# Attention of image 1 with 32 value columns in four column groups, and its row sums by way of GpSimd additions

## The reference, cut to what matters

```
g = layernorm(x)                       # per image and channel
q, k, v = w1 g + b1, w2 g + b2, w3 g + b3
scores = q^T k                         # 4096 x 4096 per image
probs  = exp(scores - rowmax(scores))
out    = (probs v) / (probs 1)         # 32 channels, and one sum per query
x      = x + g + out
```

## Time and profile before

| | |
|---|---|
| time, median of 3 runs | 1299.03 us (1297.82 to 1301.66) |
| profiled execution: span | 1557.5 us |
| profiled execution: own time beside its span | the page gives none |
| TensorE busy | 1255.7 us (81%) |
| VectorE busy | 993.9 us (64%) |
| ScalarE busy | 662.7 us (43%) |
| GpSimd busy | 485.1 us (31%), nothing after 1160 us |
| mean granted TensorE clock | 0.875 |
| attention of image 1 in the profile | 1252.7 us to the end |

### The profile page before, as it was taken

The page is one execution under the profiler, slowest core; times in us unless marked ns, Lnnn a source line. Parts: engine busy times, 40 slices in busy tenths (PEclk is TensorE's granted clock), DMA queues, the critical chain, the costliest instruction groups (busy, mean ns, idle before and its releaser), DMA issues.

```text
span 1557.5 us, 20328 instructions
## 1 busy us (share of the span) xinstructions
PE 1255.7 (81%) x7126; PEld 508.6 (33%) x7126; DVE 993.9 (64%) x1679; ACT 662.7 (43%) x882; POOL 485.1 (31%) x537
## 2 busy tenths in 40 slices
PE   5999977387879888672587767876889999999996
PEld 1888843143423333220122222222222222222221
DVE  5899988253635544463464647665687777777772
ACT  5777766243424433111032322332346544444444
POOL 6000000746464565474655354654400000000000
PEclk9999978688988988755587779888999999999999
DMA  2655401543332331111111111111000000000000
GB/s 55 156 121 119 105 1 55 170 124 104 100 99 94 100 104 36 34 44 34 44 36 36 28 39 30 40 37 30 29 0 1 0 1 14 1 0 0 0 0 14
DMA packets 59672, 79.21 MB, mean 51 GB/s; under 512 B 12230, under 2 KB 43974, under 8 KB 59414
## 3 DMA queue, kind: packets, MB, share of 16 engines
q1 hardware_dynamic: 44342, 47.03, 11.6%
q0 software_dynamic: 15264, 31.29, 7.1%
HBM read 70.94 MB, written 7.34 MB: 50 GB/s over the span
## 4 chain that ended last, share of the span: by engine, by line
PE 58%; DVE 16%; another core or an unknown queue 12%; issue 9%; ACT 3%; SPq 1%; DVEq 1%; DMA 0%; ACTq 0%
PE psum L1971 11%; PE psum L1833 9%; PE psum L1953 9%; PE psum L1994 7%; PE psum L1718 5%; DVE maxes L1144 4%; DVE probs_and_weighted L881 3%; PE psum L1733 3%; PE psum L1668 2%; PE psum L1916 2%; PE psum L1745 2%; PE psum L1843 1%; PE psum L2000 1%; PE psum L1805 1%
## 5 line engine op out<-in xcount | busy, mean ns | idle before, releaser
L554 POOL DMA_INDIRECT tile_data<-quad_table,index_u x477 | 461.4, 967 | 626.0 <-DMA quad_table<-quad_rows_or_splits 245.2
L1144 DVE TENSOR_REDUCE maxes<-psum 128x1 f32<-128x512 f32 x512 | 331.1, 683 | 172.7 <-PE psum L1953 108.5
L1574 ACT ACTIVATE quads<-psum 128x1024 f32<-128x1024 f32 x256 | 248.2, 1021 | 329.8 <-PE psum L2000 214.8
L1971 PE MATMUL psum<-quads 128*64 128x512 f32 x1024 | 277.1, 637 | 0.0
L1833 PE MATMUL psum<-scratch,quad_rows_or_splits 128*128 128x512 f32 (+1 forms) x486 | 233.8, 626 | 33.2 <-DVE scratch L966 23.4
L1953 PE MATMUL psum<-products_or_attention 128*128 128x512 bf16 x256 | 101.5, 452 | 134.4 <-DVE maxes L1144 123.3
L1994 PE MATMUL psum<-quads,probs_and_weighted 32*128 32x512 f32 x1024 | 159.8, 696 | 2.6 <-ACT quads L1574 1.8
L1833 PEld LDWEIGHTS psum<-scratch,quad_rows_or_splits 128*128 128x128 f32 x486 | 96.3, 211 | 146.6 <-issue 126.4
L978 DVE TENSOR_TENSOR probs_and_weighted<-psum,quads 128x512 f32<-128x512 f32 (+1 forms) x81 | 50.6, 640 | 145.6 <-remote 80.2
L1433 ACT ACTIVATE vals<-psum 96x384 f32<-96x384 f32 x53 | 25.8, 487 | 222.9 <-remote 96.6
L1953 PEld LDWEIGHTS psum<-products_or_attention 128*128 (+1 forms) x256 | 20.8, 99 | 266.4 <-DVE maxes L1144 176.3
(11 more groups left out here) (227 smaller groups left out, 1464.9 us busy)
## 6 DMA issues: line engine op xcount, KB each, us to landing
products_or_attention<-positions SPq DMA_DIRECT2D x30, 576.0 KB, 8.2
products_or_attention<-bands SPq DMA_DIRECT2D x12, 768.0 KB
tile_data<-quad_table,index_u POOLq DMA_INDIRECT x477
quads<-bands SPq DMA_DIRECT2D x6, 768.0 KB
quad_table<-quad_rows_or_splits SPq DMA_DIRECT2D x4, 768.0 KB, 5.6
products_or_attention<-bands SPq DMA_DIRECT2D x4, 576.0 KB
quad_table<-quad_rows_or_splits SPq DMA_DIRECT2D x2, 640.0 KB, 7.3
products_or_attention<-positions SPq DMA_DIRECT2D x4, 288.0 KB, 7.0
```

Of the source, the lines that this page charges most:

```text
L554: pool.indirect_dma_start(out=out[:, k * CORNERS * C:(k + 1) * CORNERS * C], out_offset=None, in_=table, in_offset=bass.IndirectOffsetOnAx ...
L1144: v.reduce_max(maxes[:, tile_of_q, block_of_k:block_of_k + 1], psum[:, FREE + c % 2, :], AXIS_X)\
L1574: act.activation(probs[:, s % 2, 2 * BLK * h:2 * BLK * (h + 1)], psum[:, SCORES + 2 * h:SCORES + 2 * h + 2, :].rearrange("p a n -> p (a n) ...
L1971: last = pe.matmul(psum[2 * C * h:2 * C * h + 2 * C, SUMS, :], f3[b][:, 4 * s + i, :], probs[:, s % 2, BLK * i:BLK * i + BLK], start=s == ...
```

## The change

Only image 1 is touched.

- `weigh`: each of the four key tiles' products now has a 32-column weight (values only) and its own column group (32 i). The halves and the chunks between them stay where they are.
- Behind the second half, eight products with a 32-column weight of ones, 128 queries wide: four column groups by two, over `pair_probs`. These are two sums of two key tiles each, which GpSimd adds from the probabilities (one 128 x 1024 addition a step). The products wait for that addition, and `summed` is signalled behind them.
- `copy_sums` copies a third piece (128 x 128 totals); a new `move_parts` on ScalarE at step 2 brings pieces onto the same partitions in five copies. VectorE does one reciprocal of 128 x 128 in place of four of 32 x 128, and the quotient's steps are an addition (64 x 512), an addition, a product and an addition (32 x 512 each), at steps 1, 5, 6 and 7.
- The fill of the block after the next moves from step 1 to step 7 on TensorE, from step 2 to 7 on ScalarE and from step 3 to 7 on VectorE, and uses another bank, since the old one now holds the sums with ones.

```diff
+            def add_pairs(n, u):
+
+                pool.wait_ge(probs_ready, lin(n, 2, 2 * KEY_QUADS * NBLK + 2))
+                pool.wait_ge(summed, lin(n, 1, KEY_QUADS * NBLK - 1))
+                pool.tensor_tensor(pair_probs[:, u, :], probs[:, u, 0:2 * BLK], probs[:, u, 2 * BLK:4 * BLK], ALU.add)\
+                    .then_inc(pairs_added, 1)
+
+            with pool.Fori(0, KEY_QUADS * NBLK // 2) as i:
+                for u in range(2):
+                    add_pairs((i, 2, u), u)
...
+            def pair_sum_part(j, k):
...
+                if k == 0:
+                    v.wait_ge(sums_copied, lin(j, 1, NBLK + 1))
+                    v.reciprocal(inverses, totals).then_inc(sum_steps, 1)
+                    v.tensor_tensor(att_sum[:, 0, :], att_halves[:, 0, :], att_halves[:, 1, :], ALU.add).then_inc(sum_steps, 1)
+                elif k == 4:
+                    v.wait_ge(parts_moved, lin(j, 1, 1))
+                    v.tensor_tensor(num, att_sum[0:C, 0, :], upper_sum, ALU.add).then_inc(sum_steps, 1)
+                elif k == 5:
...
+                    v.tensor_tensor(quotient, num, inverse_row, ALU.mult).then_inc(sum_steps, 1)
+                elif k == 6:
...
-                    if ahead and s == (3 if b else KEY_QUADS - 1):
+                    if ahead and s == KEY_QUADS - 1:
                         read_fill(b, fill_ahead(b, j), (var, stp, start + 2))
...
-                act.activation(att_halves[:, 1, :], psum[2 * C:4 * C, SUMS, :], ACT.Identity).then_inc(sums_copied, 1)
+                last = act.activation(att_halves[:, 1, :], psum[2 * C:4 * C, SUMS, :], ACT.Identity)
+                if b:
+                    last = act.activation(totals, psum[:, SAMPLES, 0:P], ACT.Identity)
+                last.then_inc(sums_copied, 1)
+
+            def move_parts(j):
+
+                act.wait_ge(sum_steps, lin(j, PAIR_STEPS, SUM_STEPS * NBLK + 2))
+                act.activation(upper_sum, att_sum[IMAGE[1], 0, :], ACT.Identity)
+                for g in range(4):
+                    last = act.activation(inverse_row[:, P * g:P * g + P], inverses[C * g:C * g + C, :], ACT.Identity)
+                last.then_inc(parts_moved, 1)
...
+                    if s == 2 and not first and before(b, j)[0]:
+                        move_parts(before(b, j)[1])
-                    if ahead and s == (2 if b else KEY_QUADS - 1):
+                    if ahead and s == KEY_QUADS - 1:
                         take_fill(b, fill_ahead(b, j), (var, stp, start + 2))
...
+                if b:
+                    for h in range(2):
+                        i = 2 * half + h
+                        pe.matmul(psum[C * i:C * i + C, SUMS, :], f3[b][:, 4 * s + i, 0:C],
+                                  probs[:, s % 2, BLK * i:BLK * i + BLK], start=s == 0, stop=s == KEY_QUADS - 1)
+                    if half:
+                        pe.wait_ge(pairs_added, lin((var, KEY_QUADS * stp, KEY_QUADS * start + s), 1, 1))
+                        for h in range(2):
+                            for g in range(4):
+                                last = pe.matmul(psum[C * g:C * g + C, SAMPLES, 0:P], ones[:, 0:C],
+                                                 pair_probs[:, s % 2, BLK * h + P * g:BLK * h + P * g + P],
+                                                 start=s == 0 and h == 0, stop=s == KEY_QUADS - 1 and h == 1)
+                        last.then_inc(summed, 1)
+                    return
...
-                    if ahead and b == 0 and s == KEY_QUADS - 1:
-                        pe.wait_ge(maxed, lin((var, stp, start + 1), MAXIMA, MAXIMA))
+                    if ahead and s == KEY_QUADS - 1:
+                        pe.wait_ge(maxed, lin((var, stp, start + 1 + NBLK * b), MAXIMA, MAXIMA))
                         fill(b, fill_ahead(b, j), (var, stp, start + 2))
...
-                    if ahead and b and s == 1:
-                        fill(b, fill_ahead(b, j), (var, stp, start + 2))
```

More of the change, by code:

```diff
@@ L192, in build @@
         att_halves = scratch[0:2 * C, 4 * BLK:6 * BLK].rearrange("p (h n) -> p h n", h=2)
+        at = N // 2
+        pair_probs = tile_data[:, at:at + 4 * BLK].rearrange("p (u n) -> p u n", u=2)
+        at += 4 * BLK
+        totals, inverses = (tile_data[:, at + k * P:at + (k + 1) * P] for k in range(2))
+        at += 2 * P
+        upper_sum, inverse_row = (tile_data[0:C, at + k * BLK:at + (k + 1) * BLK] for k in range(2))
         band_pos, band_int, band_floor, band_no = (y_all[:, at:at + BLK] for at in (5 * CO, 5 * CO + BLK, N + 5 * CO, N + 5 * CO + BLK))
@@ L264, in build @@
         sums_copied = sem("sums_copied"); sum_steps = sem("sum_steps"); residuals = sem("residuals_added")
-        x_final = sem("x_final")
+        x_final = sem("x_final"); pairs_added = sem("pairs_added"); parts_moved = sem("sum_parts_moved")
         block = ctx.enter_context(nc.Block())
@@ L272, in build @@
         N_CONST = 16 * (9 * DEFORMS + 11)
-        NM_STEPS, SUM_STEPS = 5, 6
+        NM_STEPS, SUM_STEPS, PAIR_STEPS = 5, 6, 4
         def lin(n, scale=1, off=0):
@@ L1166, in negated @@
                     .then_inc(nm_ready, 1)
+            def pair_sum_part(j, k):
+                var, stp, start = j
+                steps_done = SUM_STEPS * NBLK
+                num, quotient = att_sum[0:C, 1, :], att_sum[IMAGE[1], 2, :]
+                if k == 0:
[6 more added lines that the diff above has]
+                elif k == 5:
+                    v.wait_ge(sum_steps, lin(j, PAIR_STEPS, steps_done + 3))
+                    v.tensor_tensor(quotient, num, inverse_row, ALU.mult).then_inc(sum_steps, 1)
+                elif k == 6:
+                    v.wait_ge(sum_steps, lin(j, PAIR_STEPS, steps_done + 4))
+                    at = lin(j, BLK)
+                    here = slice(at, at + BLK) if isinstance(at, int) else bass.ds(at, BLK)
+                    v.tensor_tensor(x_of[1][:, here], x_of[1][:, here], quotient, ALU.add).then_inc(x_final, 1)
             def sum_part(b, j, k):
+                if b:
+                    pair_sum_part(j, k)
+                    return
                 q = queries(b, j)
@@ L1602, in attention @@
                         attend(b, (0, 0, j), last=j == NBLK - 1)
-                    act.wait_ge(sum_steps, SUM_STEPS * (NBLK * B - 2) + 1)
                     copy_sums(b, (0, 0, NBLK - 1))
+                    move_parts((0, 0, NBLK - 1))
             other_quads(0, lambda: copy_offsets_0(0, 0))
```

4 lines of the change are left out of this document (3 added, 1 removed).

## The result

The change makes the kernel slower, by about as much as forecast. After: 1314.59 us (median of 4 runs, 1313.61 to 1316.59); before, run beside it: 1300.35 us (4 runs, 1297.82 to 1304.42); ratio 1.0111, 95% interval 1.0095 to 1.0126, so +14.2 us. The profiled execution has a span of 1312.8 us and took 1314.73 itself. In the traces image 1's attention, from the first scores of its first block to the end, takes 304.8 us before (1252.7 to 1557.5) and 318.7 after (994.1 to 1312.8). The 13.9 us between them are nearly the whole difference of the medians, 14.2. The 258 us by which the profile of before was too long lie outside this stage.

A forecast was written before the change was run, and what follows sets the result against it. TensorE was taken to bound image 1's attention (39.2 of 40 us busy). Five loop blocks +10.2, first block +1.2, block 6 +2.6, last block 0 and tail +1.8 gave +15.8 us: 1299.0 becomes 1314.8, range 1304 to 1336.

The forecast's parts named there:

- block 0: Image 1's first block, weighing image 0's last step in its step 0: 3.1 - 0.98 - 0.32 - 0.62 = +1.2 us.
- block 6: Image 1's block without a fill or a stall today: 3.5 - 0.98 - 0.38 + 0.5 = +2.6 us.
- the last block with the tail: End of image 1: last block 0, since the addition fits under its 3.44 us step; tail +1.8 us.
- The ones: New TensorE products behind the second half: 0.44 us a step, 3.5 in eight steps; bounds 0.2 and 1.7.
- The values: Four column groups save 0.98 us in step 7 only; elsewhere just shorter weight loads, 0.38 us a block.
- The stall: TensorE's wait for VectorE leaves step 4 (0.62 us) and moves to step 2, charged 0.5; net -0.1.
- The fill: Moved to step 7: costs TensorE 1.05 us in either place, so nothing, with 0.2 to 0.4 us of cover.
- GpSimd's 2.5 us: One 128 x 1024 addition a step on GpSimd takes 2.5 us, hidden in the seven blocks with chunks.
- GpSimd late: Rival: the addition lasts 6.4 us and steps 6.5 rather than 5.1, giving 1421 us; chance 0.07.
- The groups running past a chunk: Faster rival: second half's products run beside the first's despite the chunk between; -40 us, 1275; chance 0.06.
- The ones hidden wholly: Faster rival: products with ones hide under the second half, which leaves two groups free; -24 us, 1291; chance 0.06.
- The contention: Rival: GpSimd's addition holds VectorE's two-SBUF-input operations; at worst 49 us, a third showing +16, 1331; chance 0.10.

The follow-up runs named there:

- one_product_with_ones: The changed kernel with seven of the eight products with ones left out a step; 1307.06 us, ratio 1.0046 to the kernel before.
- two_column_groups: The changed kernel with the four value products in two column groups rather than four; 1320.73 us, ratio 1.0154 to the kernel before.
- fill_at_step_7: The kernel before with only the fill, ScalarE's copies of it and VectorE's rest moved to step 7; 1294.32 us, ratio 0.9956.
- free_groups_sums_placed: ones_in_free_groups with VectorE's three closing operations moved right behind the first reduction of steps 4, 5 and 6; 1294.75 us, ratio 0.9959 to the kernel before.
- two_additions_a_step: The changed kernel with each GpSimd addition made twice, the first into unused space; 1392.1 us, ratio 1.0702 to the kernel before.
- the small addition: ones_in_free_groups and values_chunk_ones with GpSimd adding 64 columns instead of 1024; 1292.03 us and 1274.30 us.
- ones_in_free_groups: The changed kernel with each half given the ones products of the two column groups it leaves free; 1307.02 us, ratio 1.0059 to the kernel before.
- values_chunk_ones: The changed kernel with four value products together, then one chunk, the ones, remaining chunks, in image 1; 1307.25 us, ratio 1.0062 to the kernel before.
- halves_together: The changed kernel with the chunk between the halves moved behind them, in image 1 only; 1306.39 us, ratio 1.0057 to the kernel before.

## Why the prediction was right, point by point

**The total and its sign.** Forecast +15.8 us and 1314.8, measured +14.2 and 1314.59. That the total came so close is in part luck, since errors of both signs cancel. By the traces the five loop blocks grew by 8.7 for a forecast 10.2 and block 0 by -0.3 for 1.2; block 6, and the last block with the tail, grew by 0.6 each more than forecast. The mechanism, more work on the engine that bounds the stage, holds.

**The ones, 0.44 a step, less two shorter weight loads of 0.027 each: right.** The forecast net is 0.39; steps 3, 5 and 6 grow by 0.39, 0.38 and 0.38. `one_product_with_ones` gives the 0.44 by taking it away: 5.09 to 4.65. I had half of the records slipping under the second half as a bound of 0.2 a step. Half of them do start there, but the step still grows by the time of the busiest groups, which was the term used.

**The values: nothing in seven steps, 0.98 in step 7: right in kind.** `two_column_groups` puts it at 0.85. Of the old 1.97 us in step 7, 0.10 was waiting for the maxima and not products; that part I mis-sized. In block 6 the term fails: step 7 grew by 0.07 where -0.54 was forecast (-0.98 and +0.44), because 0.53 us of what is saved is spent waiting for the parts of the maxima. In the loop blocks the moved fill covers that wait.

**The stall: right in place, slightly too dear.** It moved from step 4 to step 2, with 0.35 idle (0.41 by the steps' difference) for a forecast 0.5.

**The fill: mis-sized in my kernel's favour.** I said that it costs TensorE 1.05 in either place. It costs 0.70 at step 7, as `fill_at_step_7` shows, because it fills 0.35 us of waiting that I had not read in the earlier trace rows. The cover of 0.2 to 0.4 us for what stands behind it held: neither the row of maxima nor the fill's rest made a wait. With these, a loop block: 2.75 for the ones in steps 0 to 6, -0.44 for values and ones together in step 7, -0.35 for the fill, -0.63 and +0.41 for the stall, together +1.74 where I had +2.0.

**The first and last blocks.** Block 0 came out at 39.49 against 39.77, not +1.2. Of that, 1.48 us is step 0 alone (6.78 before, 5.30 after). In the trace of before it runs at a lower clock, as the busy time of that stretch shows:
```profile
1254.70:1258.80 4.10, 3.96 (x11) 0.72 (x11) 1.87 (x4) 1.42 (x2) 0.00 (x0) 0.59 0.01 2
```
After, the same stretch has full clock; without that the term is +1.2, as forecast. What decides it I can't say: the profiles of `two_column_groups`, `one_product_with_ones` and `free_groups_sums_placed` show 6.8 there too, those of `fill_at_step_7` and `two_additions_a_step` 5.3. Block 6 grew by 3.16 for a forecast 2.6, by its step 7. The last block and the tail grew by 2.36: the tail's 1.92 for a forecast 1.8, and 0.43 in steps 3 and 4 of the last block, which I had at nothing. 0.30 of it stays when the addition is small, so that it is `move_parts`, for which the next probabilities wait on ScalarE. The rest, 0.12 in step 4, goes with the small addition and also with a single product with ones; TensorE waits 0.63 us for GpSimd there, whose addition takes 2.83.

**GpSimd's 2.5 us: right.** 2.35 measured. The Trainium skill, GPSIMD Engine Reference, section 3.1, would make it 2.25 by half of its figure for 2048 f32; the trace is 4% above.

**The rivals.** GpSimd late did not happen in the blocks with chunks; in the last block TensorE waits for it, which I had named as a sign of being wrong, but no more than that 0.12 us comes of it before the tail. `two_additions_a_step` shows what lies beyond the deadline, and it is worse than my rule for it (1392 where 1338 was expected of that run), because VectorE is held as well. The groups running past a chunk: no, the 5.09 in both kernels with two and four groups excludes it. The ones hidden wholly: not in this order, but in another, as `ones_in_free_groups` shows. The contention was the rival that I priced wrongly in kind. Its mechanism is real, and the price is no third of anything: it is the rest of the addition at the moment when VectorE's operation starts. In the changed kernel VectorE comes first with L1205, by 0.22 us and in one block by 0.04, and pays 0.1 with L1197 (0.79 for 0.68), which starts just before an addition's end. So my forecast held by a margin that I had not worked out, and that is luck. With steps 0.4 us shorter VectorE comes second, and most of the gain of the steps is gone.

The Trainium skill, GPSIMD Engine Reference, section 1, says that GpSimd's SBUF interfaces are shared with VectorE and that VectorE's instructions with two SBUF inputs or in a 2-port mode contend. The traces agree as to two SBUF inputs: held were L1183, L1205, L1197 and L1200. With one SBUF input, the copy of the queries and a small scalar operation (L1178 of `two_additions_a_step`, 2.10 for 0.17) were held too; whether these run in a 2-port mode no run here shows. Reductions from PSUM (0.68), the reciprocal (0.94) and L1121 with one SBUF input (0.75) were not.

## What to carry to other kernels

When an idle engine is given work, list the operations of its neighbour that share its way to SBUF, and lay both out in time: what counts is not only how busy either is but which starts first, and a margin of 0.2 us is none. If a variant that should save a fixed time per step saves nothing, compare the steps one by one; here most showed the gain, and the one or two at the block's edge gave it back. Try the parts of a change by themselves: one of them, the moved fill, was a gain of 0.4% within a change that lost 1.1%.

## What was not expected of the hardware

- Some operations of VectorE that begin while GpSimd adds are held until that addition ends, however small they are: 0.23 to 2.26 us for 128 x 16, 0.68 to 2.70 for 32 x 512, 0.43 to 2.48 for a copy of 128 x 512. What it costs is the rest of the addition. An operation of 32 x 512 that begins 0.20, 1.27, 1.67 or 2.11 us into the addition takes 2.69, 1.61, 1.21 or 0.79 us, and so always ends 0.54 behind it. Where VectorE's 0.68 us start first, GpSimd's 2.35 becomes 2.67, or 2.85 if VectorE is ahead by only 0.04.
- Matmuls in column groups that are free start beside those ahead of them in the code's order, if the shape is the same (8 of 16 records with ones, 0.02 us behind the second half's first pair). Where each half has only the products with ones of the groups that it leaves free, these cost nothing (5.09 to 4.65 us a step). A product over the whole array between two groups of products ends the overlap (5.09 with two and with four groups for the values).
- A wait of 2 us on TensorE was followed by a stretch at a granted clock of 0.50 in some cases and not in others: behind two of the five waits of `ones_in_free_groups`, behind every such wait of `values_chunk_ones`, and behind none in the loop blocks of `halves_together`.
